# Layer norms that subtract the mean as the aggregation leaves it, in two buffers by turns

## The reference

```python
def _layernorm(x, axis=-1, eps=1e-05):
    m = jnp.mean(x, axis=axis, keepdims=True)
    v = jnp.var(x, axis=axis, keepdims=True)
    return (x - m) / jnp.sqrt(v + eps)

# stage 1: 16 heads, keys of 16, values of 64; the softmax runs over the query positions
attn = softmax(einsum('bnkh,bmhk->bnhm', q, k) / 4, axis=1)
x = x + einsum('bnhv,dhv->bnd', einsum('bnhm,bmhv->bnhv', attn, v), output_proj)
# stage 2: queries from layernorm(x), keys and values from the context (64 positions),
# each through the feature map [exp(z), exp(-z)], z = x @ fm_w.T + fm_b per head
x = x + cross_attention(ctx, ctx, _layernorm(x)) @ fc_w.T + fc_b
# stage 3: y = layernorm(x), y_prev is y one position earlier
x = x + sigmoid(mix(mu_r) @ W_r.T) * (square(relu(mix(mu_k) @ W_k.T)) @ W_v.T)
```

## Time and profile before

| | us |
|---|---|
| median of 3 runs | 444.62 (443.23 to 445.12) |
| the profiled execution's own time | 445.27 |
| its span, first to last instruction | 443.5 |
| TensorE busy in it | 427.9 |
| VectorE busy | 368.4 |
| ScalarE busy | 301.4 |
| GpSimd busy | 155.2 |

### The profile page before, as it was taken

The page is one execution under the profiler, slowest core; times in us unless marked ns, Lnnn a source line. Parts: engine busy times, 40 slices in busy tenths (PEclk is TensorE's granted clock), DMA queues, the critical chain, the costliest instruction groups (busy, mean ns, idle before and its releaser), DMA issues.

```text
span 443.5 us, 8230 instructions
## 1 busy us (share of the span) xinstructions
PE 427.9 (96%) x2738; PEld 277.4 (63%) x2738; DVE 368.4 (83%) x672; ACT 301.4 (68%) x760; POOL 155.2 (35%) x200
## 2 busy tenths in 40 slices
PE   7999999999989999999999999999999999989888
PEld 5745463566546766576656685475665775568766
DVE  6788786979998889688999988799999888488875
ACT  4778986786796776657796577766877658428621
POOL 2171301137044343428242430734632532255410
PEclk9999999999999999999999999999999999979999
DMA  8668122715110002751103003443112000000001
GB/s 286 234 204 269 46 98 94 261 71 182 59 47 1 1 1 97 260 191 48 49 1 120 0 14 130 143 153 135 35 35 75 2 1 1 0 25 2 0 26 47
DMA packets 22177, 38.23 MB, mean 86 GB/s; under 512 B 2808, under 2 KB 7160, under 8 KB 21880
## 3 DMA queue, kind: packets, MB, share of 16 engines
q1 hardware_dynamic: 22136, 37.71, 25.1%
HBM read 23.02 MB, written 14.68 MB: 85 GB/s over the span
## 4 chain that ended last, share of the span: by engine, by line
PE 75%; DVE 9%; issue 6%; ACT 5%; POOL 3%; DMA 1%; SPq 0%; ACTq 0%; POOLq 0%; DVEq 0%
PE av_bank L913 22%; PE m_bank L845 8%; PE s_pair L899 8%; PE m_bank L849 6%; PE m_bank L1058 3%; ACT e_sb L1165 3%; PE m_bank L965 3%; DVE nmax L1369 3%; PE m_bank L1123 2%; PE m_bank L1070 2%; PE m_bank L1134 2%; PE m_bank L1145 2%; PE m_bank L983 2%; PE m_bank L930 1%; PE m_bank L1087 1%
## 5 line engine op out<-in xcount | busy, mean ns | idle before, releaser
L1165 ACT ACTIVATE e_sb<-s_pair,nmax 128x512 f32<-128x512 f32 x256 | 173.4, 690 | 61.6 <-DVE nmax L1369 59.8
L1369 DVE TENSOR_REDUCE nmax<-s_pair 128x2 f32<-128x1024 f32 x128 | 152.6, 1213 | 22.9 <-PE s_pair L899 21.8
L913 PE MATMUL av_bank<-e_sb,v_sb 128*64 128x512 f32 x512 | 119.0, 600 | 0.7 <-POOL v_sb L1649 0.7
L1649 POOL TENSOR_TENSOR v_sb<-v_sb,rsum 128x256 f32<-128x256 f32 x64 | 39.3, 617 | 140.4 <-DVE rsum L1377 135.7
L913 PEld LDWEIGHTS av_bank<-e_sb,v_sb 128*64 128x64 f32 x512 | 33.1, 136 | 61.6 <-issue 55.9
L899 PE MATMUL s_pair<-q_st,k_st 64*128 64x512 f32 x256 | 50.4, 457 | 3.3 <-ACT e_sb L1165 3.3
L1165 ACT ACTIVATION_READ_ACCUMULATOR e_sb<-s_pair,nmax 128x1 f32 x256 | 53.0, 207 | 0.0
L899 PEld LDWEIGHTS s_pair<-q_st,k_st 64*128 64x128 f32 x256 | 21.0, 184 | 36.7 <-ACT e_sb L1165 25.9
L1658 POOL TENSOR_TENSOR rstd<-veps,power 128x2 f32<-128x2 f32 x24 | 17.3, 719 | 58.6 <-DVE veps L1433 58.6
L845 PE MATMUL m_bank<-wo_hi,ot_hi 128*128 128x256 f32 x128 | 36.6, 291 | 0.0
L849 PE MATMUL m_bank<-wo_lo,ot_hi 128*128 128x256 f32 x128 | 34.9, 279 | 0.0
(11 more groups left out here) (182 smaller groups left out, 829.9 us busy)
## 6 DMA issues: line engine op xcount, KB each, us to landing
q_st<-q_parts SPq DMA_DIRECT2D x31, 256.0 KB, 3.4
k_st<-k_parts SPq DMA_DIRECT2D x31, 256.0 KB, 3.1
k_parts<-qkt_hi SPq DMA_DIRECT2D x7, 512.0 KB, 3.1
k_parts<-qkt_lo SPq DMA_DIRECT2D x7, 512.0 KB, 4.2
q_parts<-qkt_hi SPq DMA_DIRECT2D x8, 256.0 KB, 2.0
q_parts<-qkt_lo SPq DMA_DIRECT2D x8, 256.0 KB, 2.3
out<-x_sb SPq DMA_DIRECT2D x8, 256.0 KB, 2.2
x_sb<-in_x SPq DMA_DIRECT2D x3, 512.0 KB, 5.4
```

Source lines behind the costliest of these rows:

```text
L913: mm = pe.matmul(av_bank[n % AV_BANKS][64 * par:64 * par + 64, :], v_sb[:, m, 2 * p + par, :], e_sb[:, (4 * q + 2 * i + par) % E_RING, :], ...
L1165: act.activation(e_sb[:, g % E_RING, :], s_pair[k // 2][:, k % 2, :], ACT.Exp, bias=nmax[:, g % 8:g % 8 + 1], accum_out=esum[:, q % 4, k:k ...
L1369: dve.tensor_reduce(nmax[:, at:at + 2], s_pair[i][:, :, :], AX_X, ALU.max, negate=True)\
L1649: pool.tensor_tensor(v_sb[:, m:m + 2, 2 * p:2 * p + 2, :], v_sb[:, m:m + 2, 2 * p:2 * p + 2, :], rsum[:, q % 4, :].rearrange("p (m h) -> p ...
```

## The change

The instruction that writes the negated mean goes, and its tile with it. The normalisation subtracts the mean where `mv` holds it. `mv` now has two buffers taken by turns, as `veps` and `rstd` have. Order tables, waits and engines are as before.

```diff
-        mv = [sb("mv1", [P, 2, 2]), sb("mv23", [P, 2, 2])]
-        nmean = [sb("nmean1", [P, 2, 2]), sb("nmean23", [P, 2, 2])]
+        mv = [sb("mv1", [P, 2, 2, 2]), sb("mv23", [P, 2, 2, 2])]
...
                 ins = eng.tensor_scalar(xn_at(k, b, half)[:, t2, :], x_sb[:, x_at(b, half) + t2, :],
-                                        nmean[i][:, count % 2, t2:t2 + 1], rstd[i][:, count % 2, t2:t2 + 1],
-                                        ALU.add, ALU.mult)
+                                        mv[i][:, count % 2, t2, 0:1], rstd[i][:, count % 2, t2:t2 + 1],
+                                        ALU.subtract, ALU.mult)
...
-                        ins = dve.bn_aggr(mv[i][:, t2, :], stats[i][:, t2, :])
+                        ins = dve.bn_aggr(mv[i][:, count % 2, t2, :], stats[i][:, t2, :])
                     link(ins)
-                    dve.tensor_scalar(nmean[i][:, count % 2, :], mv[i][:, :, 0], -1.0, None, ALU.mult)
-                    dve.tensor_scalar(veps[i][:, count % 2, :], mv[i][:, :, 1], EPS, None, ALU.add).then_inc(var_ready[i], 1)
+                    dve.tensor_scalar(veps[i][:, count % 2, :], mv[i][:, count % 2, :, 1], EPS, None, ALU.add).then_inc(var_ready[i], 1)
```

## The result

The changed kernel is slower: 454.51 us, the median of 4 executions (451.37 to 457.08), against 444.87 (443.23 to 445.53) for 4 of the kernel before. The ratio is 1.0212, with a 95% interval of 1.0171 to 1.0254. The forecast was 444.2 with a range to 446.2, so both the time and the sign were wrong. The profiled execution took 455.6 us, 10.3 more than the one before.

A forecast was written before the change was run, and what follows sets the result against it. It took TensorE, busy 96% of the span and 75% of the chain, as the bound; 0.32 us from batch 3's norms plus 0.08 at 197.10 took the median from 444.62 to 444.2 us, a faster kernel; range 442.4 to 446.2.

The forecast's parts named there:

- the price of the operation on GpSimd: GpSimd's 36 normalisation instructions: subtract-and-multiply taken as 554 ns plus 1.4%, 8 ns more each, nothing on the path.
- the upper end: Upper bound for one subtract-and-multiply of 256 elements on GpSimd: 0.92 us, as a single multiplication takes.
- The slow subtraction: Rival on GpSimd: each norm ends 0.74 us later, 1.51 us in sum, 445.7 us; chance 0.14.
- The three places that it named: Where the slow subtraction would delay TensorE: 204.47 us (+0.74), 103.70 (+0.49) and 46.34 (+0.28).
- The others have 0.8 us or more: Slack given to GpSimd's remaining norms before TensorE needs them, so a slow subtraction would cost nothing there.
- A second stretch at half speed: Rival: TensorE's clock also falls in the waits from 430 to 434 us, 2.9 us slower, 447.1; chance 0.04.
- the mechanism of batch 3: TensorE's granted clock falls to 1.2 GHz from 395 to 401 us, after TensorE was busy only 2.92 of 5 us.
- The gain of 0.40 us: Removed VectorE instructions: 0.08 us at each of batch 3's four norms and at most 0.08 at 197.10.
- the fifth place, at 197: Batch 1's second norm: GpSimd's power at 197.10 and its run to 204.47 start 0.08 us earlier, TensorE follows.
- The buffers: Second buffer for mean and variance: no wait added, moved or lost, no transfer or queue touched, so no cost.

The follow-up runs named there:

- the run of the forms: The kernel before with 44 extra GpSimd instructions after VectorE's work, timing operation pairs and forms; 256 elements: add-multiply 0.55 us, subtract-multiply 1.22 us; its total is not comparable.
- The run with these two norms alone: The kernel before with subtraction only in GpSimd's back-to-back norms ln3(0,0) and ln1(2,1), nothing removed: 448.38 us, ratio 1.0068.
- the run with 16: The changed kernel with 16 matmuls of the identity by itself, results thrown away, ahead of TensorE's wait at 164 us: 455.44 us, ratio 1.0228.

## Why the prediction was wrong

**The step that failed is the price of the operation on GpSimd**: "I take 554 plus 1.4%, as subtraction stands to addition in two rows of the same kind, which is the nearest row of the operation itself". It is 1224 ns, above even the 0.92 us that stood as the upper end. The rows compared were of two tensors, where the operation indeed makes no difference (0.72 us each in the run of the forms). The instruction at issue applies a pair of operations with two scalars, and there the pair decides. The earlier trace rows held the warning: a single multiplication at 924 ns against 554 for two operations suggests that the pair of add and multiply is a special case. The prediction saw that "the form of the operation does matter" and then took the value from the other form. Between ends that far apart the nearer row was the one of the same instruction with another operation, though it too was 0.3 us short.

**The rival's mechanism was right, its size was not.** The slow subtraction stood among the rivals, with a chance of 0.14. The three places that it named are three of the five where TensorE waits. With 0.67 us for an instruction instead of 0.37, 1.34 a norm, its own working gives 1.34 less the slacks of 0.46, 0.25 and nothing: 0.88, 1.09 and 1.34. The steps in the table are 0.69, 1.24 and 1.46.

**It counted the slack norm by norm.** "The others have 0.8 us or more" fails at 164 us: GpSimd's end is 0.67 us before TensorE's transpose there (158.80 and 159.47 in the kernel before), but the norm ahead of it on GpSimd is late by 1.34 too. 2 x 1.34 - 0.67 = 2.0, and 2.04 was measured. The run with these two norms alone lost 2.8 us, the slow clock included; exchanging them halved the wait. The last wait, 0.49 at 194, is a matter of size: the slack there was 0.78 us (185.49 and 186.27 in the kernel before), more than the rival's 0.74 and less than 1.34.

**A second stretch at half speed was a rival, in the wrong place.** It was looked for from 430 us, by the mechanism of batch 3. It came behind the longest new wait, at 165, and cost 1.6 us in the profiled execution. The executions of the changed kernel spread over 5.7 us in step with the mean granted clock: 451.37 at 1.00, 453.43 at 0.996, 455.6 at 0.989 and 457.08 at 0.985. Only the profiled one shows where its stretches lie, so how much of that spread lies behind new waits is not known.

**The gain of 0.40 us** was about right in its unit: 0.06 to 0.07 us from norm to norm in batch 3, against the 0.08 that was read from two starts. No run shows the sum of 0.40, and the fifth place, at 197, was not measured. The Trainium skill, "VectorE: DVE Perf Modes", section "The DRAIN you can't avoid", would by its main rule, that the pipeline must be empty first, have made it 0.17 each. The same section lets a next instruction that is not held start earlier, and these rows agree with that.

**The buffers** were costed at nothing: "no transfer or queue is touched". Their places alone cost 1.1 us in the kernel before, and less in the changed one. No row of before could have sized that, but a bound of nothing was too firm for a change that alters what is allocated.

In sum, for the profiled executions: waits for GpSimd 6.6 us (4.5, 2.3 less the 0.7 of before, 0.5), the slow clock 1.6, the start's transfers 0.6: 8.8 of 10.3. What is left is 1.5 us. The longer matmuls explain at most 1.1 of it, the figure of the other kernel, and the removed work should have taken some 0.3 off (an estimate: 0.07 at each of five norms). The rest is not placed.

## What to carry to other kernels

Before an operation of an instruction is exchanged for one that is its equal in arithmetic, time that very instruction with that very pair on that engine; durations of another instruction of the same engine did not carry over here. When an engine's work gets longer, add up the delay over everything that it does without a pause and set the sum against the first consumer, instead of giving each piece its own slack. And where buffers are added or removed, keep the places of the others, or the measurement mixes two changes.

## What the runs showed of the hardware that was not expected

GpSimd has two speeds for a pair of operations with scalars per partition. On 256 elements add-multiply, multiply-add and multiply-multiply take 0.55 us, and the five other pairs tried 1.22 or 1.23; by the three sizes that is 0.8 ns for each element with add-multiply and 3.3 with subtract-multiply. A single operation (0.92 us) is slower than a fast pair of two. With constants instead of scalars from memory, add-multiply takes 0.40, subtract-multiply 1.07 and a single operation 0.85. The Trainium skill, "GPSIMD Engine Reference", section 4.1, calls one-input work of this engine roughly line-rate. The fast pairs may be what it describes; the four-fold rate between pairs disagrees with it as a rule.

TensorE's matmuls of 256 columns in the output projection run at 291 or 292 and 278 or 279 ns (the two largest groups), or at 294 and 281, by where the buffers lie, in the profile of every one of the seventeen kernels run. Those of the cross-attention's output projection do the same, 287 or 288 against 292 ns (but for the profiles of the changed kernel and of the two norms, where a half-speed stretch lies in that group). The weights `wo_hi` and `wo_lo`, of 256 columns, lie at the same addresses in all the programs as built; `ot_hi` and `ot_lo`, which are loaded against them, lie 64 bytes lower in the slower set, with all other buffers behind `veps`. Which of these addresses makes the difference was not tried.

A multiplication of 128 float32 columns by a float32 identity showed as two rows, 32 for 16 instructions, and took 0.22 us of TensorE (3.57 us for 16 on the chain of the run with 16) at the full clock.
